# GpSimd waits for its row transfers to land at every fourth of them

## What is computed

```python
logits = x @ gate_w.T
w, sel = jax.lax.top_k(jax.nn.softmax(logits), 8)
w = w / jnp.sum(w, axis=-1, keepdims=True)
pos = ...                      # the token's place in its expert's queue, over all batches
slot = jnp.where(pos < 64, pos, 64)
xin = zeros((64, 65, 256)).at[eid, slot].set(x[tok])
h = silu(xin[:, :64] @ wg) * (xin[:, :64] @ wu)
out = h @ wd
y = zeros(...).at[tok].add(out[eid, slot] * w)
x = _layernorm(x + y)
```

## Time and profile before

| | us |
|---|---|
| median of 3 runs (366.66 to 368.79) | 367.25 |
| the profiled execution's own time | 367.73 |
| its span, first to last instruction | 365.8 |
| PE busy (share of the span) | 268.9 (74%) |
| DVE busy | 229.8 (63%) |
| GpSimd busy | 168.1 (46%) |
| ACT busy | 142.8 (39%) |
| 48 row transfers, L548, 990 ns each | 47.5 |
| 16 row transfers of batch 3, L561, 975 ns each | 15.6 |
| 32 scatters, L643, 1547 ns each | 49.5 |

### The profile page before, as it was taken

The page is one execution under the profiler, slowest core; times in us unless marked ns, Lnnn a source line. Parts: engine busy times, 40 slices in busy tenths (PEclk is TensorE's granted clock), DMA queues, the critical chain, the costliest instruction groups (busy, mean ns, idle before and its releaser), DMA issues.

```text
span 365.8 us, 5569 instructions
## 1 busy us (share of the span) xinstructions
PE 268.9 (74%) x1825; PEld 170.5 (47%) x1825; DVE 229.8 (63%) x533; ACT 142.8 (39%) x258; POOL 168.1 (46%) x179
## 2 busy tenths in 40 slices
PE   8668888898899878897888756663699999940000
PEld 4455546666476555674556444332354545520000
DVE  0928763789768697787725663811577777720792
ACT  4610582259642298422873242100144444430021
POOL 2003022400537627556353571777055788873272
PEclk9896999999999999999599986595599999985555
DMA  7789515699963315378133893193489997656981
GB/s 240 256 246 314 159 48 156 172 309 383 373 186 109 112 52 157 87 234 315 52 93 112 228 324 106 33 260 68 136 232 316 170 161 116 70 62 123 366 299 57
DMA packets 47262, 66.68 MB, mean 182 GB/s; under 512 B 5981, under 2 KB 33244, under 8 KB 47234
## 3 DMA queue, kind: packets, MB, share of 16 engines
q1 hardware_dynamic: 38544, 56.07, 49.6%
q0 software_dynamic: 7680, 9.47, 14.0%
q10 hardware_dynamic: 1010, 0.80, 0.8%
HBM read 36.52 MB, written 28.75 MB: 178 GB/s over the span
## 4 chain that ended last, share of the span: by engine, by line
PE 42%; DVE 24%; issue 9%; ACT 8%; another core or an unknown queue 7%; DMA 5%; POOL 1%; SPq 1%; ACTq 1%; POOLq 0%; DVEq 0%
PE M L1430 14%; PE O L1430 9%; PE SB L1430 6%; DVE nmax L995 6%; PE SA L1430 5%; PE O L1933 3%; DMA acc_d<-xp_t,idx_out 2%; ACT probs L684 2%; DVE early L1390 2%; DMA early<-acc_d 2%; DVE early L1396 1%; DMA early<-weights 1%; ACT early L684 1%; DVE early L1006 1%
## 5 line engine op out<-in xcount | busy, mean ns | idle before, releaser
L548 POOL DMA_INDIRECT xin_d<-row,idx_slot x48 | 47.5, 990 | 31.5 <-issue 13.7
L643 POOL DMA_INDIRECT acc_d<-xp_t,idx_out x32 | 49.5, 1547 | 26.6 <-DVE idx_out L1334 17.4
L1430 PE MATMUL M<-middle 128*128 128x256 f32 (+3 forms) x144 | 28.6, 388 | 5.8 <-DVE middle L1245 2.4
L884 ACT ACTIVATE xp<-M 128x96 f32<-128x96 f32 x32 | 8.0, 251 | 52.5 <-remote 25.6
L1430 PEld LDWEIGHTS M<-middle 128*128 128x128 f32 (+1 forms) x144 | 20.3, 199 | 14.1 <-issue 8.0
L1430 PE MATMUL SA<-early 96*128 96x256 bf16 (+1 forms) x128 | 21.1, 291 | 5.4 <-ACT early L774 3.4
L1339 DVE COPY xp_t<-O 128x256 f32<-128x256 f32 x32 | 13.6, 424 | 17.4 <-remote 16.5
L602 POOL TENSOR_TENSOR early<-early 128x1024 f32<-128x1024 f32 x3 | 6.4, 2144 | 39.1 <-ACT early L694 39.1
L1430 PE MATMUL SB<-early 96*128 96x256 bf16 (+1 forms) x128 | 21.0, 290 | 2.8 <-ACT probs L684 0.9
L995 DVE TENSOR_REDUCE nmax<-SB 128x4 f32<-128x1024 f32 x16 | 19.5, 1220 | 3.8 <-PE SB L1430 3.2
L1430 PE MATMUL O<-middle,early 128*128 128x256 f32 (+1 forms) x96 | 21.3, 368 | 0.8 <-DVE middle L1035 0.6
(11 more groups left out here) (279 smaller groups left out, 641.7 us busy)
## 6 DMA issues: line engine op xcount, KB each, us to landing
acc_d<-zeros SPq DMA_DIRECT2D x3, 2176.0 KB, 17.1
early<-acc_d SPq DMA_DIRECT2D x24, 256.0 KB, 6.0
early<-early SPq DMA_DIRECT2D x44, 128.0 KB
xin_d<-zeros SPq DMA_DIRECT2D x1, 5136.0 KB, 19.5
early<-wgu SPq DMA_DIRECT2D x12, 384.0 KB
middle<-wgu SPq DMA_DIRECT2D x12, 384.0 KB
probs<-xin_d SPq DMA_DIRECT2D x20, 160.5 KB
gu_sb<-wgu SPq DMA_DIRECT2D x8, 384.0 KB, 7.1
```

Source lines behind the costliest of these rows:

```text
L548: nc.gpsimd.indirect_dma_start(xin_d, bass.IndirectOffsetOnAxis(ap=idx[:, t, k:k + 1], axis=0), rows[:, t, 0:ROW], None, bounds_check=SLOT ...
L643: nc.gpsimd.indirect_dma_start(acc_d[p % CHAINS], bass.IndirectOffsetOnAxis(ap=idx_out[:, p:p + 1], axis=0), yw[:, p % YRING, :], None, bo ...
L884: nc.scalar.activation(htanh[:, p % 2, :], M[:, p % 2, 0:INNER], ACT.Tanh, scale=0.5).then_inc(S["htanh"], 1)
L1430: return nc.tensor.matmul(o, l, r, start=start, stop=stop)
```

## The change

Before each row transfer of `into_slots` whose count n is a multiple of 4 (but 0), GpSimd waits until all n transfers before it have landed. Before the first transfer of `last_into_slots` it waits for all 48, and before each further group of four for the four before.

```diff
+IN_A_ROW = 4
...
+            sent_so_far = itertools.count()
+
             def into_slots(b, idx, rows, tiles, ranks=range(TOPK)):
                 for t in tiles:
                     for k in ranks:
+                        n = next(sent_so_far)
+                        if n > 0 and n % IN_A_ROW == 0:
+                            pool.wait_ge(S["slotted"], 16 * n)
                         nc.gpsimd.indirect_dma_start(
...
             def last_into_slots(b):
                 for k in range(TOPK):
                     for t in range(NT):
+                        if t == 0 and k == 0:
+                            need(pool, "slotted", b - 1)
+                        if t == 0 and k % 2 == 0 and k > 0:
+                            pool.wait_ge(S["ranks"][k // 2 - 1], 16 * IN_A_ROW)
```

More of the change, by code:

```diff
@@ L14 @@
 from contextlib import ExitStack
+import itertools
 import concourse.bass as bass
```

## The result

The changed kernel takes 380.7 us (median of 4 runs, 377.8 to 386.0) where the kernel before takes 368.0 beside it (4 runs, 366.7 to 370.3). The ratio is 1.029, with a 95% interval of 1.022 to 1.036. It is slower by 11 us by the ratio and by 13 us by the medians, and lies outside the predicted range of 360.0 to 371.5 us. The profiled execution is one of 378.1 us with a span of 376.2, against 367.73 and 365.8 before: 10.4 us to account for. Its lines are numbered 3 to 12 higher than those of before (L548 is L556, L561 is L573, L1177 is L1189, L1339 is L1351).

What follows compares the result with a forecast made beforehand. Bound: PE and DVE in turn, with waits for PE after long runs of GpSimd's row transfers, and GpSimd's scatters at the end. Terms -5.5 + 2.8 = -2.7 us gave 365.0 profiled, 364.5 us median; range 360.0 to 371.5.

Steps and rivals of the forecast that it cites:

- The stalls: Waits for PE after long transfer runs: pauses give back 2.8 and 2.7 us in the middle iterations, 6.7 in the last batch.
- the stalls stay: Rival: stalls come from PE's own work, not the transfers, so only the cost is left; 370.0 us, chance 0.20.
- The pauses there at nothing: Middle iterations (2, 1, 3) and (3, 2, none): pauses cost nothing, covered by GpSimd's waits, leaving the gain of -5.5 us.
- The last batch: Pauses reach the path: n = 36 at 217.0, n = 40 at 225.1, SP's first load of rows +3.0 us.
- The rival of quick landings: Landings are quick throughout, so the last batch keeps 3 us of its gain; 358.8 us, chance 0.10.
- The scatters set the end, so the whole stage costs +2.8: Start of the pair loop: scatter 0 starts no earlier than 269.8 instead of 267.01, delaying the end by 2.8 us.
- Sum: Whole kernel: -5.5 us in the middle iterations and +2.8 us for the later stage make -2.7 us.
- this bound: Last run: the two stalls' 16.5 us gain is lost to batch 3's transfers ending 13.2 us later; scatter 0 +2.8 us.

Runs made afterwards that it cites:

- e1: Changed kernel with pauses only at n = 4 to 28, in the two middle iterations; ratio 0.992 to the kernel before.
- e11: Changed kernel without the four pauses of batch 3; 371.9 and 372.7 us, beside 371.4 for the kernel before.
- e16: The changed kernel unaltered, run once more on the fourth set's chip; 376.4 us in one execution, beside 368.7 for the kernel before, 1.02.
- e7: Changed kernel with pauses at n = 4 to 36 only and the last batch's norm steps behind n = 39 and 40; ratio 1.029 to the kernel before.
- e2: Changed kernel with pauses only from n = 32 on and in the transfers of batch 3; ratio 1.013 to the kernel before.
- e3: Changed kernel with pauses only before and in batch 3's 16 transfers; ratio 1.017 to the kernel before.
- e4: Changed kernel with pauses only at n = 36, 40 and 44, around the last batch's two norm steps; ratio 1.020 to the kernel before.
- e9: The kernel before, unaltered, profiled once more on the third set's chip; 375.96 us in this one execution, beside 371.4.
- e12: Changed kernel with pauses only at n = 4 and n = 20; 369.7 and 370.2 us, beside 371.4 for the kernel before.
- e8: The changed kernel unaltered, on the second set's chip, where nothing is heard late; 380.1 us, ratio 1.084 to the kernel before.
- e13: Changed kernel with a GpSimd power of 1.4 us in place of each of 16 pauses; 364.6 us, ratio 0.990 to the kernel before.
- e10: Changed kernel with one small memset in place of each pause, on a chip with late signals; ratio 0.999 to the kernel before.
- e5: Changed kernel with one small memset in place of each pause, on a chip without late signals; 349 us, ratio 0.993 to the kernel before.
- e6: Changed kernel with eight small memsets in place of each pause, on a chip without late signals; 351 us, ratio 1.001 to the kernel before.

## Why the prediction was wrong

**The stalls.** Right: PE is heard late in long runs of row transfers, and pauses end it. 2.8 and 2.8 us came back at L1177 and, the second time, at L986 too (predicted 2.8 and 2.7), 6.4 in the last batch (6.7), and L1339's waits went. The rival "the stalls stay" is refuted. The rule of the Trainium skill beside it, "SBUF — State Buffer", section "SBUF: two separate sides", is about the ports of SBUF; these runs don't refute it, it only doesn't tell when PE is heard. In other executions with the same middle pauses (e1, e11, e16) one wait near 195 us stayed 0.9 to 2.2 us late, so "end it" holds for the first trace and "most of it" for all.

**"The pauses there at nothing."** This step failed, by 7.9 us. I had looked at who waits behind the pauses on GpSimd, and found cover for each: the next transfers waited for scores anyway. I had named two subtractions and a norm step behind them, and had asked only whether these come late for someone. They don't. They come late enough to meet other operations of VectorE, at 140 and at 195 us. Each meeting costs VectorE 2.4 us, and in this trace PE's clock falls behind each. These two are 4.9 of the 7.9 us, and eight matmuls at half the clock 1.8 more; the rest isn't taken apart. In all six traces with pauses at n = 8 and 12 (the changed kernel three times, e1, e7, e11) the operation near 140 took 3.46 to 3.65 us; the one near 195 took 0.69 to 3.14, by the chance of a us. Without these pauses (e2, e3, e4, e9) or with one in their place (e12) the one near 140 took 1.2. The clock doesn't always fall with it: from 145 to 150 us the granted clock was 0.50 to 0.67 in four of the six traces, and 1.00 in e8 and e11.

The result does not hang on the first pair of traces. From one place in the start-up (VectorE's L1170, at 38.82 us before) to n = 32, four traces without middle pauses on chips with late signals (the first, e2, e3, e4) took 167.5 to 170.2 us, and two with them (the first of the changed kernel, e11) 169.9 and 169.1. A gain of 5.5 us is in neither.

**The last batch.** Each pause was sized well. Counted from the batch's start, n = 36 starts at 217.6 (predicted 217.0), n = 40 at 224.3 (225.1), and the stage up to scatter 0 costs 3.1 us (2.8). Put at 5.7 and 2.0 us, the pauses took 6.4 to 7.1 and 1.9. The rival of quick landings falls.

**"The scatters set the end, so the whole stage costs +2.8."** The shift was right, the rest was not: 3.1 us more are lost between scatter 0 and the end. PE was held by pairs 5 to 7 and fell to 1.2 GHz, and the rows, weights and scatters that had been held back came together. Taking a stage behind a delay as merely shifted left this out. Of its size only this much is known: 3.1 us between the first two traces, and 9.7 more in e8, where PE stays at 1.2 GHz far longer.

**Sum.** 7.9 + 0.3 + 3.1, and 1.8 us at the start make the 13.1 us between -2.7 and +10.4. The 1.8 us are chance: at this place the same kernel in e8 is 0.2 us ahead of the kernel before, and e4, which has no pause before n = 36, is 1.7 us behind it.

**Deeper than the terms.** The sum set a gain of 16.5 us in the last run against GpSimd's 13.2 us and let both vanish at scatter 0. The table above shows that this bound was sound on such a chip. But the gain exists only on some chips. On one without late signals the changed kernel is 30 us slower than the kernel before. I took a wait with an unknown releaser for a property of the kernel. No trace of one execution could have told otherwise, but it was reason enough for a wider range. Nor had I asked whether the landing matters: it is the price of a pause beside weight loads, and most of the cure needs only the gap.

**Open.** Why PE is heard late at all, and why on some chips only; whether it is the chip or how the program was placed on it. Why PE stays at 1.2 GHz for over 30 us of full work in some executions. The parts measured alone (0.992 and 1.013) make 1.005 where the whole is 1.029 on another chip (and 1.02 in e16's one execution); L1090's collision, which e1 didn't have, is 2.4 us of these 9, the rest isn't explained.

## What to carry to other kernels

When an edit delays an engine, look not only at who waits for it but at what its own arithmetic will now run beside: a GpSimd operation that moves by 2 us can triple a VectorE operation with two inputs (1.21 us became 3.61 here), and PE, which then waits, may go on at half its clock. When waits for matmuls have an unknown releaser, compare on another chip before building on them, and take away the suspected cause as cheaply as can be (a gap of 1.5 us) rather than with a wait for a landing that lasts 6 to 8 us beside bulk loads. An engine with a stream of its own at the end, as the scatters here, pays every pause in full as soon as the stalls that hid it are gone.

## What the hardware showed that was not expected

- Behind six or more of GpSimd's indirect transfers in a row, 1.28 us apart, engines that wait for PE go on late on some chips: 1.1 us behind six (e12), and with waits of up to 10.4 us, remote, in longer rows (the kernel before). A gap after every fourth takes most of it away, 1.9 us of waiting or 1.6 of arithmetic. What is left behind four in a row is one wait in each of e1, e11 and e16 and two in e13, 0.9 to 2.2 us late. An instruction of 0.13 us between two transfers leaves them 1.28 us apart and the lateness where it was (e10).
- The lateness was there in every trace with long runs where the kernel before took 368 to 373 us (medians), and in none of the three with long runs (e5, e6, e7) where it took 351. Chip and placement of the program were not told apart.
- A small operation of GpSimd behind a transfer costs nothing: it fits in the 0.30 us that stands between two transfers anyway (0.13 us, e10).
- A pause for landing takes 1.9 to 2.6 us on queues that are idle or nearly so and 5.7 to 7.8 beside weight loads. The Trainium skill, "DMA: Bandwidth & Descriptors", section "Anatomy of one DMA — SWDGE (gpsimd) path", has a fixed cost of about 2.0 us per transfer, to which the time to move the bytes is added. The idle case agrees; the other is some three times that and more.
- With GpSimd's operation of 2.1 us beside it, VectorE's 1.21 us took 3.46 to 3.65 and its 0.69 us up to 3.14, though by the records VectorE's started first.
- PE, busy without a break from 280 to 310 us, ran at 1.2 GHz all of that time in one execution of the changed kernel (e8) and at 0.92 of full speed in another, with 132 and 212 matmul records.
